# One layer of a decoder on one core: the first normalisation on ScalarE, u behind the first two maxima, the cut of k ahead of a recurrence product, and V's projection in one place

## What is computed

```python
u  = (conv + 1) * x                       # conv: a complex recurrence over the 32 sequences
x1 = (u - mean(u)) / sqrt(var(u) + 1e-5)
q, k, v = relu(x1 @ Wq + bq), relu(ctx @ Wk + bk), relu(ctx @ Wv + bv)
p  = softmax(q @ k.T / 4)                 # per head, 16 heads of 16 numbers
x2 = layernorm(x1 + ln_g * norm(p @ v + q) + ln_b)
xn = scale * x2 * rsqrt(mean(x2**2) + 1e-6)
e  = argmin(distance(xn, centroids))      # one of 8 experts per vector
out = layernorm(2 * x2 + expert_e(xn))
```

## Time and profile before

| | before |
|---|---|
| median of 3 runs | 1281.18 us (1277.73 to 1294.08) |
| the profiled execution | 1285.39 us |
| its span, first to last instruction | 1283.3 us |
| PE, DVE, ACT, POOL busy | 1114.9, 953.8, 664.2, 792.0 us |
| mean granted clock of PE | 0.935 of full speed |
| exponentials, line 559 | 512 of 595 ns |
| maxima, line 888 | 512 of 682 ns |

### The profile page before, as it was taken

How to read it: one execution, slowest core, us unless ns; L and a number is a source line. 1 busy time by engine, 2 the same in 40 slices (tenths; PEclk the granted TensorE clock), 3 DMA queues, 4 the chain that set the end, 5 groups by cost and what they waited for, 6 DMA issues and landing times. The chain is left out here.

```text
span 1283.3 us, 27523 instructions
## 1 busy us (share of the span) xinstructions
PE 1114.9 (87%) x8060; PEld 817.8 (64%) x8061; DVE 953.8 (74%) x2411; ACT 664.2 (52%) x1413; POOL 792.0 (62%) x943
## 2 busy tenths in 40 slices
PE   0599999999999998999999999830999999999996
PEld 0465666666666666666666666520788888888885
DVE  6357799899899899899899898639455555555553
ACT  1247577676677677776776677514322222222221
POOL 6545778888788888888887865344133333333333
PEclk9859899999899999999999999755999999999998
DMA  5556755655556646656556555206011111111110
GB/s 143 131 158 173 189 144 143 154 138 150 141 142 149 160 130 153 151 146 155 142 146 152 141 134 128 76 25 180 25 53 49 44 52 49 52 46 47 53 49 22
DMA packets 90827, 144.92 MB, mean 113 GB/s; under 512 B 12663, under 2 KB 78336, under 8 KB 84513
## 3 DMA queue, kind: packets, MB, share of 16 engines
q1 hardware_dynamic: 84192, 126.61, 38.3%
q0 software_dynamic: 6528, 16.99, 4.5%
HBM read 91.44 MB, written 53.03 MB: 113 GB/s over the span
## 5 line engine op out<-in xcount | busy, mean ns | idle before, releaser
L888 DVE TENSOR_REDUCE neg_max_sb<-S 128x2 f32<-128x512 f32 x512 | 327.9, 682 | 78.6 <-PE S L693 77.6
L559 ACT ACTIVATE probs<-T 128x512 f32<-128x512 f32 x512 | 278.5, 595 | 152.4 <-PE T L706 140.5
L693 PE MATMUL S<-k_st,q_st 48*128 48x256 f32 x1024 | 215.4, 320 | 51.5 <-DMA k_st<-k_pieces 26.0
L693 PEld LDWEIGHTS S<-k_st,q_st 48*128 48x128 f32 x1024 | 146.7, 193 | 131.1 <-issue 56.3
L706 PE MATMUL T<-q_st,k_st 49*128 49x256 f32 x1024 | 210.5, 318 | 3.7 <-ACT probs L559 2.1
L706 PEld LDWEIGHTS T<-q_st,k_st 49*128 49x128 f32 x1024 | 145.6, 192 | 21.0 <-ACT probs L559 16.2
L1201 ACT ACTIVATE gT<-GT 128x512 f32<-128x512 f32 x71 | 42.6, 600 | 207.5 <-PE GT L1236 207.5
L669 PE MATMUL O<-probs,v_aug 128*32 128x256 f32 x2048 | 147.1, 408 | 0.7 <-ACT probs L559 0.7
L1177 POOL DMA_INDIRECT out<-res,token x71 | 76.4, 1076 | 101.5 <-DVE res L1309 101.5
L1258 PE MATMUL Y<-dn_sb,gT 128*128 x568 | 134.2, 379 | 0.8 <-ACT gT L1201 0.8
L513 POOL DMA_INDIRECT buckets<-row,slot x64 | 66.2, 1034 | 90.4 <-DVE slot L1052 80.2
(11 more groups left out here) (177 smaller groups left out, 2551.6 us busy)
## 6 DMA issues: line engine op xcount, KB each, us to landing
q_st<-q_pieces SPq DMA_DIRECT2D x64, 256.0 KB, 4.7
k_st<-k_pieces SPq DMA_DIRECT2D x64, 256.0 KB, 5.9
xr<-buckets SPq DMA_DIRECT2D x71, 129.0 KB, 2.1
xt<-in_x SPq DMA_DIRECT2D x32, 256.0 KB, 6.4
ct<-in_ctx SPq DMA_DIRECT2D x32, 256.0 KB, 6.8
up_sb<-in_L_ffn_up_w SPq DMA_DIRECT2D x8, 1024.0 KB, 8.6
q_pieces<-q_hi SPq DMA_DIRECT2D x32, 256.0 KB, 2.1
q_pieces<-q_lo SPq DMA_DIRECT2D x32, 256.0 KB, 2.1
```

Of the source, the lines that this page charges most:

```text
L559: a_.activation(probs[:, h % 8].rearrange("p k t -> p (k t)"), T_ps[h % 2][:, :], ACT.Exp, scale=DH ** -0.5).then_inc(s["exp_ok"], 1)
L693: last = t_.matmul(S_ps[h % 2][:, c * TOK:(c + 1) * TOK], q_st[base:base + STACK, h, c * P:(c + 1) * P], k_st[base:base + STACK, h, :], st ...
L888: v.tensor_reduce(neg_max[:, cur.mod(2), :, h], S_ps[h % 2][:, :].rearrange("p (c t) -> p c t", c=NTC), AX.X, ALU.max, negate=True).then_i ...
```

## The change

x1 leaves DVE: ACT computes it as rs*u + shift at h = 13, behind v_aug, with one activation per chunk, and DVE makes the small tile shift = -mean*rs at h = 10. u goes from h = 3 to h = 0, ahead of `row`; its statistics go to h = 2, both stages together. The second half of V's projection goes from h = 12 to h = 11, next to the first. On POOL the cut of k changes places with the first product of `conv_imag`.

```diff
@@ POOL, step
-                    conv_imag(t + 3, 0)
                     cut(n, k32[:, :, :], k_hi, k_lo, "k_ok", "k_cut", k_out)
+                    conv_imag(t + 3, 0)
                     conv_imag(t + 3, 1)
@@ ACT, step
+                        if h == 13 and active(n + 1):
+                            nn = n + 1
+                            wait(act, "shift", nn)
+                            wait(act, "y_ok", nn - 4, 4)
+                            for c in range(NTC):
+                                a_.activation(x1[:, nn.mod(4), c], u[:, c], ACT.Identity, bias=shift[:, c:c + 1],
+                                              scale=rs1[:, 1, c:c + 1]).then_inc(s["x1_ok"], 1)
@@ PE, step
-                        if h in (11, 12) and active(n):
-                            c = h - 11
+                        if h == 11 and active(n):
...
+                            t_.matmul(M_ps[1][:, :], ones_bf[:, :], bv_cut[:, :], start=True, stop=False)
+                            for c in range(NTC):
+                                for ic in range(NCH):
...
+                                last.then_inc(s["v_pe"], 1)
@@ DVE, step
+                        if h == 0 and active(nn):
+                            wait(dve, "x1_ok", nn - 1, 2)
+                            wait(dve, "conv", nn, 5)
+                            wait_ring(dve, x_in[nn.mod(2)], nn, 2, 16)
+                            v.scalar_tensor_tensor(u[:, :, :], state[:, 0], 1.0, xt[:, nn.mod(2)], ALU.add, ALU.mult).then_inc(s["u_ok"], 1)
                         if h == 0 and active(b):
...
-                        if h == 3 and active(nn):
...
-                        if h == 4 and active(nn):
+                        if h == 2 and active(nn):
                             wait(dve, "u_ok", nn)
                             wait(dve, "rstd1", nn - 1, 2)
                             stats(nn, u, st1, "ln1")
+                            moments(nn, st1, mv1, "ln1")
...
-                            if active(nn):
-                                moments(nn, st1, mv1, "ln1")
...
+                        if h == 10 and active(nn):
+                            wait(dve, "rstd1", nn, 2)
+                            v.scalar_tensor_tensor(shift[:, :], mv1[:, :, 0], -1.0, rs1[:, 1], ALU.mult, ALU.mult).then_inc(s["shift"], 1)
...
-                        if h == 13 and active(nn):
-                            wait(dve, "rstd1", nn, 2)
-                            wait(dve, "y_ok", nn - 4, 4)
-                            for c in range(NTC):
-                                v.tensor_scalar(x1[:, nn.mod(4), c], u[:, c], mv1[:, c, 0:1], rs1[:, 1, c:c + 1],
-                                                ALU.subtract, ALU.mult).then_inc(s["x1_ok"], 1)
```

More of the change, by code:

```diff
@@ L143, in build @@
             rs1 = sb1("rs1", [P, 2, NTC])
+            shift = sb1("shift", [P, NTC])
             x1 = sb1("x1", [P, 4, NTC, C])
@@ L202, in build @@
                 negT neg_ok neg_out neg_in0 neg_in1 t_pe exp_ok pv o_ev x_pe o_ok qn_pe qn_ok oq_ok lnx rstdx
[L203 removed]
+                x1b_ok y_ok ln2 rstd2 x2_ok rms xw_ok offset shift nx_ok xnT_pe xnT_ok dist_pe pick rank_pe slot_ok
                 id_ok scat0 scat1 pool_waits sp_waits dve_waits"""
@@ L501, in step @@
                         rstd(t + 2, "ln1", 4, mv1, rs1, "rstd1")
+                    cut(n, k32[:, :, :], k_hi, k_lo, "k_ok", "k_cut", k_out)
                     conv_imag(t + 3, 0)
-                    cut(n, k32[:, :, :], k_hi, k_lo, "k_ok", "k_cut", k_out)
                     conv_imag(t + 3, 1)
@@ L792, in step @@
                                 wait(pe, "o_ok", a, 4, 2)
-                            if c == 0:
-                                t_.matmul(M_ps[1][:, :], ones_bf[:, :], bv_cut[:, :], start=True, stop=False)
-                            for ic in range(NCH):
-                                last = t_.matmul(M_ps[1][:, c * C:(c + 1) * C], ctT[:, ic, c * P:(c + 1) * P], wv_sb[:, ic, :],
-                                                 start=False, stop=(c == NTC - 1 and ic == NCH - 1))
-                            last.then_inc(s["v_pe"], 1)
+                            t_.matmul(M_ps[1][:, :], ones_bf[:, :], bv_cut[:, :], start=True, stop=False)
+                            for c in range(NTC):
+                                for ic in range(NCH):
+                                    last = t_.matmul(M_ps[1][:, c * C:(c + 1) * C], ctT[:, ic, c * P:(c + 1) * P], wv_sb[:, ic, :],
+                                                     start=False, stop=(c == NTC - 1 and ic == NCH - 1))
+                                last.then_inc(s["v_pe"], 1)
                         if h == 14 and active(n):
```

6 lines of the change are left out of this document (removed).

## The result

The changed kernel takes 1307.49 us (median of 4 runs, 1302.58 to 1309.07), beside 1287.2 us of the kernel before (4 runs, 1277.73 to 1294.08). The ratio is 1.016, with a 95% interval of 1.011 to 1.021: slower, though the interval doesn't settle whether by 2%, outside the range of 1244 to 1300, and to the other side than forecast. The profiled execution is the quickest of the four, one of 1302.58 us, with a span of 1300.5 us.

What follows compares the result with a forecast made beforehand. PE's waits before S of head 0 and at K's projection, 1.56 us per step, were the winnable part. 21.30 + 0.84 + 0.49 + 0.29 + 0.4 = 23.32 against 23.87 us per step gave 1265 us, range 1244 to 1300.

Steps and rivals of the forecast that it cites:

- What bounds the kernel: Whole step of 23.87 us: 21.30 work, 1.34 and 0.22 waits, 0.72 lost to the clock, 0.29 unplaced.
- 0.29 that I couldn't place: Remainder of the 23.87 us step, 0.29 us, after work, waits and clock; kept in the forecast sum.
- the timeline's 21.30: PE from S of head 0 to the end of the last flip, nothing waited for: 21.30 us at full clock.
- u: DVE at head 0: u takes 1.0 us instead of 2.5; K's projection loses its wait of 0.22 us.
- V in one place: End of step: the maximum of head 12 starts 0.78 us later, so S of the next head 0 waits 0.84.
- The sign that I named: Profile after, DVE at head 12: DVE waits for S ahead of the maximum of head 12.
- x1 on ACT: Start of step: x1 waits for y2, the pair takes 0.84 us, the flip of x1 waits 0.49 for ctT.
- The cut of k: POOL: the load of `k_st` is done 22.20 us after the last head 0, PE arrives at 22.63: just off the path.
- The sum: Whole step: 21.30 + 0.84 + 0.49 = 22.63, with the unplaced 0.29 it is 22.92 us before the clock.
- The clock: Whole step: loss to low clock between 0 and 0.72 us, taken as 0.4, giving 23.32 against 23.87.
- Rival B: Slower, chance 0.15: waits of 0.84 and 0.49 us take the clock down every step, 1.67 us each, 1303 us.
- The ring over POOL: Theory 2 of the experiments: waits from DVE's slots through POOL's scatter, conv_input, distances and DVE's choice set the full-clock step.

Runs made afterwards that it cites:

- b_u_first: The kernel before with only u moved to head 0 and its statistics to h = 2; ratio 1.005 to the kernel before.
- a_fill: The changed kernel with three and two unread matmuls put into PE's waits before S of head 0 and the flip of x1; ratio 1.000 to the kernel before.

## Why the prediction was wrong, point by point

- **What bounds the kernel**: right in its parts (1.34 us of waits, the clock, 0.29 that I couldn't place), wrong in the weight. I read the clock's 0.72 (0.62 by the single steps) as something that comes along with the longest waits. Of the waits for DVE 3.1 us in 11 waits stood in the middle of the step, which the timeline's 21.30 may hold already.
- **u**: 0.69 us where I took 1.0; it waited for conv_input as worked out: this ended at 493.83, 2.18 us after S where I had 2.1, and DVE was idle ahead of u for 6.9 + 0.7 us in 27 steps, though the profile names POOL for the 0.7 alone. K's projection stopped waiting, as forecast. But b_u_first shows that the move is worth nothing by itself. I had given it only 0.22 us; even that went into other waits.
- **V in one place**: forecast a wait of 0.84 us before S, measured 0.80 in the 18 steps that DVE ends. The chain from the maximum of head 12 to S was right, 3.66 us for 3.73. The sign that I named, DVE idle ahead of that maximum, didn't come: in 12 steps DVE was late by its one-hot tile and began it 1.11 us after S of head 12 instead of 0.54. PE came later to its last flip by as much, so the wait was met partly by luck. Alone the move costs 2.1%.
- **x1 on ACT**: forecast 0.49 us for the flip of x1 in each step, measured 0.56 in 14 steps and 0.15 to 0.27 in five, 0.34 on average. The pair took 1.09 us against 0.84, inside the bounds, and ACT waited 24.0 us for y2, 27 times.
- **The cut of k**: said to be just off the path. In 10 of 27 steps `k_st` came last, with up to 2.4 us. Both waits of S together are (14.3 + 16.6) / 28 = 1.10 us (28 starts of a step in the window) where the sum had 0.84: 0.26 too little. The load varies more than the 6.92 us of one step told.
- **Not seen**: the one-hot tile. Beside POOL's product, which the early cut pushed to 506.90, it took 1.26 us (507.35) and ended with it at 508.6; PE waited 0.60. This is the shared port again that the Trainium skill ("SBUF — State Buffer", "SBUF: two separate sides") describes, and the trace agrees. The wait is 0.20 us per step, and DVE's delay of some 0.55 us behind it in 12 steps comes on top.
- **The sum** at full clock: forecast 22.92, which is 0.23 less than the same count gave before (23.87 - 0.72). The rest of the step in the profile after is 23.06, but that agreement is in part luck: `k_st` and the one-hot tile were missing with 0.26 and 0.20, the flip was 0.15 too dear, and the 0.29 that I couldn't place was nearer 0.1. Nor is it the length of a step at full clock: the steps that kept the clock grew from 23.48 to 23.85, and with the waits filled the step grew from 23.39 to 23.64. So this term failed too, in its direction: longer by some 0.3 where I had it shorter by 0.23.
- **The clock is the step that failed first**: 0.4 us forecast; 1.40 measured as the same count, and worth at least 24.46 - 23.85 = 0.61 by the steps that kept it and 0.82 by a_fill. The forecast itself named a granted clock below 0.95 as its undoing, and it was 0.94. 1.0 x 30 steps = 30 us, and 1265 becomes 1295; the kernel before was 1287.2 instead of 1281.2 in the session of the result, which makes it 1301 against 1307. These 30 us take the count at its full price; at 0.7 of it they are 21, and the step at full clock has to give the rest. I argued from one step, at 396.61, that kept its clock after 1.92 us of waiting. Over the 14 kernels without filler 27 steps began with 1.9 us or more, and it is the only one that kept it.
- **Rival B** named the mechanism, two short waits close together, and I gave it 0.15. It took place in 8 of 17 such steps and not in every one, and in three of the eight (515.61, 590.58, 665.68) the clock fell 0.35 to 0.47 us after S, after the wait of 0.80 alone. Its price of 1.67 us was that of one low stretch; of the 14 low steps of the changed kernel eight lost 3.3 us or more. The Trainium skill ("TensorE: Matmul & The Clock Gate", "HAM oscillation — how this bites in real kernels") tells of a kernel whose waits for DMA take the clock down in every round; here waits for VectorE and ScalarE of under a microsecond each did in some rounds, as a_fill shows.

What stays open: how much of the 1.6% is the clock and how much the step itself, beyond the bounds above; and why the steps that kept the clock stay between 23.05 and 24.01 us in all 14 kernels without filler, wherever a wait is taken away. The ring over POOL would explain where the waits reappear, and moving conv_input brought some 0.5 us in one kernel but 0.15 in the other. It is argued, not shown. Why one step keeps its clock after a wait and the next does not is open too.

## What to carry to other kernels

When an edit trades one wait of TensorE for another, price the clock with the wait: count in the trace how many steps with that much waiting were followed by a stretch at half clock, and take that share, not the best step. Length times (1 - clock) overstates the price, here by some 30%, since other waits shrink behind a low stretch. A test is cheap: matmuls into an unread bank inside the wait. If the kernel gets faster with them, the clock was the cost, and the fix may be to leave them in. A few tenths taken from a busy engine (u, 1.3 us of DVE per step) were worth nothing here; ask first whether the chain that ends in the waiting matmul gets shorter.

## What the runs showed of the hardware

- Waits of 0.80 and 0.56 us within two microseconds, with PE mostly busy for the rest of the step, came with a stretch at 1.2 GHz in 8 of 17 steps; with 1.1 us of matmuls in the waits none of 27 steps had one.
- Four unused matmuls per step in the kernel before took the counted loss to the clock from 0.62 to 0.19 us per step, and 1.1% off the time.
- An activation over 128x256 from SBUF with bias and scale by partition took 592 ns, as long as one over 128x512 from PSUM (594) and longer than one over 128x256 from PSUM (472 to 482).
- An operation of DVE with two SBUF inputs, on 16 numbers per partition, took 1.26 us instead of 0.16 to 0.2 beside a product on POOL.
